# One product in place of two comparisons: ternary weights rounded by the conversion to fp8 and clipped by a sign function

## What is computed

```python
def _bitlinear(x, w):
    scale = jnp.mean(jnp.abs(w))
    q = jnp.round(jnp.clip(w / (scale + EPS), -1.0, 1.0))
    return x @ (q * scale).T

gate  = _bitlinear(y, w_gate)       # w_gate 2752 x 1024, fp32
up    = _bitlinear(y, w_up)         # w_up   2752 x 1024
out   = x + _bitlinear(gate * up, w_down)   # w_down 1024 x 2752
```

## Time and profile before

| | |
|---|---|
| median of 3 runs | 1794.7 us (1794.46 to 1794.79) |
| the profiled execution | 1794.94 us, of which 1793.1 us are the span of the trace |
| TensorE busy | 1739.4 us, 97% of the span |
| VectorE busy | 1116.8 us, 62% |
| ScalarE busy | 544.8 us, 30% |
| GpSimd busy | 36.5 us, 2% |
| mean granted clock of TensorE | 0.991 of full speed |

### The profile page before, as it was taken

How to read it: one execution, slowest core, us unless ns; L and a number is a source line. 1 busy time by engine, 2 the same in 40 slices (tenths; PEclk the granted TensorE clock), 3 DMA queues, 4 the chain that set the end, 5 groups by cost and what they waited for, 6 DMA issues and landing times.

```text
span 1793.1 us, 29779 instructions
## 1 busy us (share of the span) xinstructions
PE 1739.4 (97%) x11897; PEld 1166.1 (65%) x11897; DVE 1116.8 (62%) x1861; ACT 544.8 (30%) x853; POOL 36.5 (2%) x62
## 2 busy tenths in 40 slices
PE   5798999999999999999999999999999999999999
PEld 3344454444546959588685968679594977768584
DVE  4999964785442646856467545855468455766464
ACT  5767441121211313332132312323132322333030
POOL 0200000110000000000000000000000000000000
PEclk8899999999999999999999999999999999999999
DMA  8546511252002302241113312142023412222021
GB/s 314 179 134 239 146 59 65 103 194 113 1 24 96 109 28 103 86 168 63 73 53 140 116 42 104 62 173 64 34 90 110 149 60 93 73 104 78 21 104 47
DMA packets 56557, 180.10 MB, mean 100 GB/s; under 512 B 6112, under 2 KB 6432, under 8 KB 56416
## 3 DMA queue, kind: packets, MB, share of 16 engines
q1 hardware_dynamic: 53712, 163.60, 26.0%
q0 software_dynamic: 2480, 14.22, 2.0%
q10 hardware_dynamic: 224, 0.28, 0.0%
HBM read 147.07 MB, written 31.01 MB: 99 GB/s over the span
## 4 chain that ended last, share of the span: by engine, by line
PE 88%; DVE 5%; issue 4%; DMA 1%; ACT 1%; SPq 1%; DVEq 0%; ACTq 0%
PE ps L777 43%; PE ps L591 23%; PE ps L834 20%; DVE msk L1274 2%; PE ps L795 2%; DMA inter<-in_L_ffn_w_gate_dram 1%; DVE msk L1278 1%; DMA bbc<-biasd 1%; DVE yp L1237 0%; SPq L469 0%; DVE wsum L1158 0%; ACT g_r L952 0%; ACT msk L952 0%; DVE prod L1306 0%; SPq L455 0%
## 5 line engine op out<-in xcount | busy, mean ns | idle before, releaser
L777 PE MATMUL ps<-yp,wgT 128*128 128x256 f16 x3528 | 773.4, 273 | 1.7 <-DVE xr L1327 1.0
L777 PE MATMUL ps<-wuT,wgT 128*128 128x256 f16 x3528 | 773.4, 273 | 0.0
L777 PEld LDWEIGHTS ps<-yp,wgT 128*128 128x128 fp8e4 x3528 | 345.3, 98 | 44.5 <-issue 3.6
L777 PEld LDWEIGHTS ps<-wuT,wgT 128*128 128x128 fp8e4 x3528 | 345.3, 98 | 41.3
L834 PE MATMUL ps<-wdT,inter 128*128 128x512 fp8e4 x1680 | 371.3, 379 | 0.0
L834 PEld LDWEIGHTS ps<-wdT,inter 128*128 128x128 f16 x1680 | 163.9, 98 | 194.7 <-issue 1.1
L1582 DVE SCALAR_TENSOR_TENSOR xr<-ps,osc,xr 128x512 f32<-128x512 f32 x180 | 134.1, 748 | 146.6 <-PE ps L834 111.5
L591 PE MATMUL ps<-yp,wgT 128*128 128x512 f16 x672 | 152.0, 385 | 2.9 <-DVE yp L1237 1.8
L1531 DVE TENSOR_TENSOR wdT<-ps,msk 128x512 f32<-128x512 f32 (+1 forms) x66 | 44.0, 666 | 177.9 <-PE ps L777 177.9
L591 PE MATMUL ps<-yp,wuT 128*128 128x512 f16 x672 | 151.5, 382 | 0.0
L591 PE MATMUL ps<-wdT,inter 128*128 128x512 fp8e4 x672 | 147.7, 379 | 0.0
(11 more groups left out here) (209 smaller groups left out, 1602.7 us busy)
## 6 DMA issues: line engine op xcount, KB each, us to landing
wgT<-wcomb SPq DMA_DIRECT2D x60, 896.0 KB, 4.6
wdT<-dcomb SPq DMA_DIRECT2D x12, 2240.0 KB, 10.3
xa<-in_x_dram SPq DMA_DIRECT2D x8, 2048.0 KB, 7.8
out_dram<-xr SPq DMA_DIRECT2D x64, 256.0 KB, 2.0
wdT<-in_L_ffn_w_up_dram SPq DMA_DIRECT2D x10, 512.0 KB, 4.2
wcomb<-raw POOLq DMA_DIRECT2D x11, 448.0 KB, 2.7
ys<-in_L_ffn_w_down_dram SPq DMA_DIRECT2D x9, 512.0 KB, 4.2
wcomb<-msk POOLq DMA_DIRECT2D x10, 448.0 KB, 2.8
```

The costliest lines, as they stand in the source:

```text
L777: last = nc.tensor.matmul(out, w, operand(i, OPERAND[what])[:, k, :], start=(start and h + k + i == 0), stop=(k == KQ - 1 and i == 1), ski ...
```

## The change

A tile is quantised by one VectorE pass. `threshold` makes `unit` = -(mean + EPS) x 512 and its reciprocal; the pass multiplies the tile by it and writes fp8. The smallest step of that format is 1/512, so that the conversion rounds `-w / (mean + EPS)` to a whole number of steps: 0 up to half, else one step or more. The values go through the transpose, and ScalarE's copy out of PSUM applies the sign function, which makes -1, 0 or 1 of them. Sums of the up tiles and of the first twelve down tiles are divided anew: of the 22 up sums VectorE has 15 instead of 5, of the twelve down sums 6 instead of 4. A wait is added ahead of the first up product of chunk 0, for the quantising of the tile that lies in `prod`.

```diff
-    on_act = [i not in SUM_DVE if i < NG else i % 4 != 1 if i < 2 * NG else
-              i % 3 != 1 if i < 2 * NG + 12 else i % 2 == 0 for i in range(NQ)]
+    on_act = [i not in SUM_DVE if i < NG else i % 3 == 0 if i < 2 * NG else i % 2 == 0 for i in range(NQ)]
...
-                    nc.scalar.copy(blocks(dst), pairs[:, :, :, 0:rows], saturate=False).then_inc(s_te, 1)
+                    nc.scalar.activation(blocks(dst), pairs[:, :, :, 0:rows], ACT.Sign, saturate=False).then_inc(s_te, 1)
...
-                V.tensor_scalar(nthr[:, m:m + 1], mean[:, m:m + 1], EPS, -0.5, ALU.add, ALU.mult)
-                V.tensor_scalar(thr[:, m:m + 1], mean[:, m:m + 1], EPS, 0.5, ALU.add, ALU.mult).then_inc(s_thr, 1)
-                dve.wait_ge(s_thr, m + 1)
+                V.tensor_scalar(unit[:, m:m + 1], mean[:, m:m + 1], EPS, -1.0 / QUANTUM, ALU.add, ALU.mult).then_inc(s_unit, 1)
+                dve.wait_ge(s_unit, m + 1)
+                V.reciprocal(per_unit[:, m:m + 1], unit[:, m:m + 1]).then_inc(s_per, 1)
+                dve.wait_ge(s_per, m + 1)
...
                 for src, dst in quantised(n):
-                    last = V.tensor_scalar(dst, src, thr[0:rows, m:m + 1], None, ALU.is_gt, saturate=False)
-                last.then_inc(s_gtv, 1)
-                dve.wait_ge(s_gtv, n + 1)
-                for src, dst in quantised(n):
-                    last = V.scalar_tensor_tensor(dst, src, nthr[0:rows, m:m + 1], dst, ALU.is_lt, ALU.subtract,
-                                                  saturate=False)
+                    last = V.tensor_scalar(dst, src, per_unit[0:rows, m:m + 1], None, ALU.mult, saturate=False)
                 last.then_inc(s_q, 1)
...
                 if u == 0:
+                    if isinstance(c, int) and c == 0:
+                        dve.wait_ge(s_q, 1 + max(n for n, e in q_load.items() if loads[e][3] == ("prod", 0)))
                     dve.wait_ge(s_gr, c + 1)
```

More of the change, by code:

```diff
@@ L38, in adaln_ternary_ffn @@
     PROD = 2.0 ** -15
+    QUANTUM = 2.0 ** -9
     EXPONENT = 0x7F800000
@@ L189, in adaln_ternary_ffn @@
         mean = sb("mean", [P, 3], f32)
-        thr = sb("thr", [P, 3], f32)
-        nthr = sb("nthr", [P, 3], f32)
+        unit = sb("unit", [P, 3], f32)
+        per_unit = sb("per_unit", [P, 3], f32)
         kk = sb("kk", [P, 3], f32)
@@ L351, in adaln_ternary_ffn @@
         s_mean = sem("s_mean")
-        s_thr = sem("s_thr")
-        s_gtv = sem("s_gtv")
+        s_unit = sem("s_unit")
+        s_per = sem("s_per")
         s_q = sem("s_q")
@@ L990, in copy_T @@
                 f0, nf = m * (CT // P), min(CT // P, FT - m * (CT // P))
-                last = nc.scalar.copy(blocks(wdT[:, f0:f0 + nf // 2 * 2, r * P:(r + 1) * P]),
-                                      pairs[:, :, 0:nf // 2, :], saturate=False)
+                last = nc.scalar.activation(blocks(wdT[:, f0:f0 + nf // 2 * 2, r * P:(r + 1) * P]),
+                                            pairs[:, :, 0:nf // 2, :], ACT.Sign, saturate=False)
                 if f0 + nf == FT:
-                    nc.scalar.copy(wdT[:, FT - 1, r * P:(r + 1) * P], pairs[:, 0, nf // 2, :], saturate=False)
+                    nc.scalar.activation(wdT[:, FT - 1, r * P:(r + 1) * P], pairs[:, 0, nf // 2, :], ACT.Sign,
+                                         saturate=False)
                     for h in range(2):
-                        last = nc.scalar.copy(wdT[h * FR:(h + 1) * FR, FT, r * P:(r + 1) * P],
-                                              pairs[0:FR, 0, nf // 2 + 1, :], saturate=False)
+                        last = nc.scalar.activation(wdT[h * FR:(h + 1) * FR, FT, r * P:(r + 1) * P],
+                                                    pairs[0:FR, 0, nf // 2 + 1, :], ACT.Sign, saturate=False)
                 last.then_inc(s_te, 1)
```

## The result

The changed kernel takes 1771.9 us (median of 4 runs, 1771.8 to 1772.3) against 1794.65 us (1794.5 to 1794.8) before: a ratio of 0.9874, with an interval of 0.9856 to 0.9891. The forecast was 1774.0 us in a range of 1771.5 to 1782.0. The direction, the mechanism and the range held; the gain, 22.8 us, is 2.1 larger than the 20.7 that were forecast (1794.7 less 1774.0).

A forecast was written before the change was run, and what follows sets the result against it. TensorE bound the kernel after 249 us; before, it waited for tiles from VectorE and ScalarE. Gains 1.9 + 8.4 + 2.7 + 8.2 = 21.2 us off 1794.7 give 1773.5, plus 0.5 for sign: 1774.0 us, range 1771.5 to 1782.

The forecast's parts named there:

- B: Most gate groups with 39 tile transposes, 62.91 to 152.57 us: all 8.4 us lost there would be gained.
- C1: First four up groups, to the down weights' total, 152.57 to 171.13 us: 2.7 us gained, a smaller wait left.
- C2: 18 more up groups with the last 25 tiles, 171.13 to 249.00 us: all 8.2 us lost there gained.
- undisturbed it is 3.98 us: TensorE's pitch for a gate group and two tiles, taken as the floor: 3.98 us.
- VectorE's load after: VectorE's work per gate group, first eleven: 3.2 us after the change, under TensorE's 3.98.
- ScalarE: Gate groups with two sums on ScalarE cost it 4.9 us, over 3.98; with at most one, 3.63 us.
- Start: Up to the second tile's transpose at 62.91 us: 1.9 us gained, first product 1.2 us earlier.
- Sign: Sign function in ScalarE's tile copies out of PSUM: 0 to 0.5 us in all, 0.5 added.
- (a): Rival: tiles come in time but TensorE's clock doesn't stay up; 1776 to 1781 us, chance 0.20.
- (b): Rival: sums or loads limit the gate groups' second half; 8 us lost, about 1782; chance 0.11 with the slow product.
- (c): Rival: ScalarE reloads function tables between sign copies and sums; about 1834 us, chance 0.04.
- (d): Rival: TensorE isn't supplied sooner, since another order holds it; about 1794 us, chance 0.03.

The follow-up runs named there:

- the first two experiments: The changed kernel with the old division of the sums, 1776.6 us; the kernel before with the new division of the sums alone, 1805.5 us.
- the first experiment: The changed kernel with the old division of the sums (5 of 22 up sums, 4 of the first 12 down sums on VectorE): 1776.6 us.

## Why the prediction was right, and where its sizes were off

- **What bounds the kernel**: right. Everything behind the up groups moved as a whole (1544.10 and 1544.24 us), and the gain is the sum of the stages ahead of it. The errors of the terms don't cancel: start and B were too small by 0.7 and 1.4 us, sign was 0.5 too dear, and C1 and C2 fit within 0.1. The page was misread by one slice: TensorE is at 8 tenths in the fourth and at 9 for good from the fifth; nothing hung on it.
- **B**: the mechanism was right for both engines, as the first two experiments show, the term was too small, 8.4 against 9.8 us. The step that failed is "undisturbed it is 3.98 us": the forecast took fifteen groups at 3.98 and three at 3.90, 71.4 us, and they took 70.3 (seventeen at 3.90 and one at 4.00); the two groups with a short operation took 7.37 us and not 7.6. The groups without a shown wait were paced by VectorE. The forecast had both clues, VectorE's 4.0 us for two tiles and the last three groups at 3.90, and took the larger value for the floor. "Below them the change can do nothing" was wrong. Of the "three waits of about 0.8 us behind ScalarE" the trace puts two down to ScalarE and the third, at 90.97, to VectorE; the first experiment shows that ScalarE alone would have cost 0.92 us there and at a fourth place that the forecast gave to VectorE.
- **VectorE's load after**: 3.2 us per group was too much; a pass adds 0.67 us in a row of its kind and a sum 1.13, which makes 2.8. That the moved sums are hidden by the freed passes and cost about 10 x 1.2 us without them was right (10.8 us), in part by luck: 7.3 us of it fell in B, and 3.9 in C1 through one long wait and the half clock behind it.
- **ScalarE**: 4.9 against 3.98 us was right, 0.92 us per such group at the new pitch. The late loads of down tiles, and the some 6 us by which they go out earlier (6.3), were right too.
- **Start**: 2.6 instead of 1.9 us. 0.35 of it is there before anything of the change runs (the first total at 50.32 instead of 50.67); counted from that total it is 2.2. The first product was 1.3 us earlier by that count, forecast 1.2: the first pass took 1.19 and not 1.33 us, and the reciprocal added 0.15 (0.57 us from mean to first tile instead of 0.42). The eight matmuls at half clock became the bound, as forecast (the second transpose follows them at 60.33 without a wait).
- **C1**: 2.6 for 2.7. From ScalarE's first high part to the total it is 10.82 us (145.27 to 156.09), 10.81 before. The remaining wait is 1.27 us, forecast 1.1.
- **C2**: 8.1 for 8.2; here the pitches of 3.68 and 4.11 us had been read where VectorE's lateness didn't show, and they stand. The added wait ahead of the first up product cost nothing: VectorE stood there for ScalarE's copy (2.11 us), not for its own tile.
- **Sign**: the added 0.5 us was not there.
- **Rivals**: (a) no clock fall followed the remaining wait; the clock mattered only at the start. Against the forecast's remark that both falls had followed two waits in a row, the new division alone has one behind the single wait of 4.95 us. (b) no sum waited long for a load: the longest such wait is 0.89 us, in C1. (c) no table was loaded. (d) fell with the result. The Trainium skill (ScalarE: Activation LUTs, Table sets: the hidden batching unit) says that cheap functions, relu, copy, identity and abs by name, are in every set of tables. The trace agrees for copy and abs, and sign, which isn't named there, behaved as they do: no load came between tile copies by sign and sums by absolute value.

## What to carry to other kernels

Before a distance between two events of the bounding engine is taken for its floor, look whether another engine runs without any idle time beside it; a pitch that equals a whole number of that engine's operations (2 x 1.99 = 3.98) may be that engine's, even where no wait is shown. A merged row that lasts longer than its like elsewhere (0.69 and 0.61 us) is the sign to look for. When a pass is taken from one engine, move work to it from the engine that would be next, in the same step: here the same redistribution costs 10.8 us alone and brings 4.0 to 4.7 beside the shorter pass. Order within a queue may count as much as load: with the old sums two of them ahead of the tile copies cost 0.92 us, and two behind them nothing, though no run moved the same two from one place to the other.

## What the runs showed of the hardware that was not expected

- Two one-source passes of VectorE in a row, fp32 to fp8 over 1024 elements, take 1.42 us and not twice 0.754; a first pass with a handoff to the second of another kind had taken 0.79 of the 1.99.
- In five kernels whose first product began at 56.8 to 57.5 us the granted clock rose from half to full at 60.3, 60.7, 61.3, 62.4 and 62.8 us; from the first product to the first whole group they took 5.5 to 6.6 us. Matmuls without use ahead of the first product kept the clock at 1.00 through it, and the time didn't move, since TensorE then waited 1.42 us for data.
- ScalarE's sign function from PSUM, fp8 to fp8 over 1024 elements, took 1.026 us, a copy of the same shape 1.019 to 1.022.
- VectorE's first pass over a tile at the start, beside GpSimd's work, took 1.19 us (1.76 with the threshold first), and the same pass later 0.75; that GpSimd is the reason wasn't tested.
